# Lambda products of two batches as one full-height matmul, in an audio tower of signatures, a lambda layer and routed experts

## The chip, the cores and the metric

The kernel runs on one core of a Trainium2 chip. The metric is the device time of one execution in microseconds; lower is better. Everything that counts here is float32 (or fp32r, the same width read by TensorE in one pass instead of two).

## What is computed

The input is x, 64 sequences of 64 points with 7 channels. Three stages follow each other:

```
h = signature_features(x) @ W.T + b            # 64 x 63 tokens, 128 features
h = h + lambda_attention(layernorm(h))          # this stage is changed
h = h + routed_ffn(layernorm(h)) + shared_ffn   # 8 experts, top 1
```

The middle one, for each batch b of 63 tokens, has one key and one value head of 16 channels and 8 query heads:

```
q = bn(x @ Wq).reshape(b, 8, 16, t);  k = softmax((x @ Wk).reshape(b, 1, 16, t));  v = bn(x @ Wv).reshape(b, 1, 16, t)
lam_c = einsum('bukt,buvt->bkv', k, v)          # 16 x 16 per batch: the product that is changed
Yc = einsum('bhkt,bkv->bhvt', q, lam_c)
lam_p = relu(conv3x3(v, Wpos));  Yp = einsum('bhkt,bkvt->bhvt', q, lam_p)
out = (Yc + Yp) reshaped @ Wout + bout
```

## The kernel before, in words

The program has three blocks with a barrier between them: `signatures`, `middle` and `experts`. Only `middle` is touched. Each engine has its own instruction stream, in an order written out by hand; semaphores join them.

**Preparation in `middle`.** The raw keys and values come back from DRAM as 128 partitions x 8 groups (`G8`) x 63 tokens, where a group is 8 batches of 16 channels: `KR`/`KS` for keys, `VR`/`VN` for values. DVE normalizes the values, subtracts the maximum of the keys and later divides by their sum; ACT does the exponential. Then TensorE turns both so that tokens lie on partitions: `turn` makes 8 transposes of 128 x 63 into two PSUM banks each. ACT copies the banks into `VT` (63 x 64 batches x 16) and `KT` (63 x 64 x 16). At the same time the padded values are written to DRAM (`v_pad`) and read back as shifted images (`load_im`, tile `IM`) for the convolution; the first one must have landed before `conv(0, 0)`.

**The main loop.** `GB` = 4 batches make a group, so there are `NG` = 16 groups, and `step(k)` runs for k = -1 to 17. It is a software pipeline: step k works on the convolution and the attention of group k, on the layer norm and the shared FFN's first product of group g = k-1, and on the FFN's second product of group f = k-2. TensorE's order in a step is: `conv(k, 1)` (L1187), the second half of the sums of products of the group before (`add_products`, L1196), `conv(k, 2)`, the output projection (L1242), `down(f)` (L1218, 16 matmuls), `rank` in odd steps (L1226), `conv(k, 3)`, the content product (L1255), a transpose (L1262), `add_products(k, 0)`, the gate (L1270), `up(g)` (L1208, 12 matmuls), the **lambda product of group k+1** (L1279), and `conv(k+1, 0)`.

**The lambda product.** ACT repeats the 16 keys of each of 4 batches over 8 heads into `KH` (L976). TensorE makes one matmul for each batch, with `KH` of that batch as weights (63 rows, 128 columns) and `VT` of that batch as moving data (63 rows, 16 columns), into `psL`; the last one increments `lam_done`. ACT waits for that and copies `psL` to `LS` (L1001), and only then goes on to the GELUs of the group before (L963, L964). GpSimd makes `Gl` from `GF` (L912), which `down` waits for, and spreads `LS` over heads into `LC` (L916), which the content product waits for.

**The convolution** has 36 rows: `W36` and `IM` lie on partitions 0-35 for two of the batches and 64-99 for the other two. DVE's `products` (L1062, four in a row) wait for it, and `conv(k, 2)` waits until the first two of them have emptied a PSUM bank.

**DVE** ends even steps from k = 2 with `choose` (L1072 to L1080), which picks each token's expert and keeps the running counts `RUN`; it is in DVE's order ahead of the `products` of the next, odd step.

Of the kernel before, what the change touches and what calls it, by code (L numbers as in the profile page):

```python
# [6 lines left out]
f32 = mybir.dt.float32  # L7
# [4 lines left out]
ACT = mybir.ActivationFunctionType  # L12
AX = mybir.AxisListType

NB, S, F = 64, 63, 128
# [3 lines left out]
DK, NH = 16, 8  # L19
# [5 lines left out]
SP = 64  # L25
# [3 lines left out]
GB = 4  # L29
# [703 lines left out]
def middle(nc, m):  # L733
# [5 lines left out]
    with ExitStack() as ctx:  # L739
        def sb(name, shape, dt=f32):  # L740
            return ctx.enter_context(nc.sbuf_tensor(name, shape, dt))
# [4 lines left out]
        G8, IC, HV, CT = NB // 8, I // 128, DK // 2, 2 * TOK  # L746
# [3 lines left out]

        flat, n_k = W2[:].rearrange("p e i h f -> p (e i h f)"), G8 * S
        KR, KS = (flat[:, n * n_k:(n + 1) * n_k].bitcast(f32).rearrange("p (g s) -> p g s", g=G8) for n in range(2))
        VR = flat[:, 2 * n_k:2 * n_k + G8 * SP].bitcast(f32).rearrange("p (g s) -> p g s", g=G8)
# [5 lines left out]
        PQ = sb("PQ", [128, 2, S])  # L759
        KT, VT = sb("KT", [S, NB, DK]), sb("VT", [S, NB, 4, 4])  # L760
        KH = sb("KH", [S, 2, GB, NH, DK])
        WPh, WPm, W36 = sb("WPh", [100, 128], f32r), sb("WPm", [100, 128]), sb("W36", [100, 128], f32r)
# [54 lines left out]
        psV = PS[7][:, 0:2 * DK].rearrange("p (a c) -> p a c", a=2)  # L817
        psKT, psVT = PS[6:8], PS[4:6]

# [71 lines left out]
        def _(pool):  # L891
            L = Links(pool, pool_link)
            for x in (VN[:, :, 0:1], VN[:, :, SP:SP + 2]):
                pool.memset(x, 0.0).then_inc(vp_set, 1)
# [47 lines left out]
        def _(act):  # L942
# [6 lines left out]
            load_im(act, 0, (1,))  # L949

            act.wait_ge(kv_done, 1)
            for h in range(2):
                act.activation(VT[:, 32 * h:32 * h + 32], psVT[h][0:S, :].rearrange("p (b r j) -> p b j r", r=4, j=4), ACT.Copy).then_inc(kvt_ready, 1)
            act.wait_ge(kv_done, 2)
            for h in range(2):
                act.activation(KT[:, 32 * h:32 * h + 32].rearrange("p b k -> p (b k)"), psKT[h][0:S, :], ACT.Copy).then_inc(kvt_ready, 1)
            act.wait_ge(kvt_ready, 4)

# [7 lines left out]
            def step(k):  # L966
# [7 lines left out]
                if on(k + 1, 0, NG):  # L974
                    wait_from_one(act, lam_done, k)
                    act.activation(KH[:, w], KT[:, (k + 1) * GB:(k + 2) * GB].unsqueeze(2).broadcast_to([S, GB, NH, DK]),  # L976
                                   ACT.Copy).then_inc(kh_ready, 1)
# [180 lines left out]
        def _(pe):  # L1158
# [8 lines left out]

            def turn(to, x, lo):
                for q in range(G8):
                    ins = pe.transpose(to[q // 4][0:S, 128 * (q % 4):128 * (q % 4) + 128], x[:, q, lo:lo + S], ident)  # L1170
                ins.then_inc(kv_done, 1)
            pe.wait_ge(vn_ready, 2)
            turn(psVT, VN, 1)
            pe.wait_ge(k_ready, 1)
            turn(psKT, KS, 0)
            pe.wait_ge(w36_ready, 1)
# [52 lines left out]
            def step(k):  # L1229
# [43 lines left out]
                if on(k + 1, 0, NG):  # L1273

                    pe.wait_ge(kh_ready, k + 2)
                    if on(g, 0, NG):
                        pe.wait_ge(lg_ready, g + 1)
                    for b in range(GB):
                        ins = pe.matmul(psL[:, b], KH[:, w, b].rearrange("p h k -> p (h k)"), VT[:, (k + 1) * GB + b].rearrange("p j r -> p (j r)"), start=True, stop=True)  # L1279
                    ins.then_inc(lam_done, 1)  # L1280
# [3 lines left out]
            conv(0, 1)  # L1284
            pe.wait_ge(kvt_ready, 4)
            for k in range(-1, NG + 2):
# [216 lines left out]
```

## Time and profile before

| | |
|---|---|
| median of 3 executions | 672.87 us (669.7 to 681.77) |
| profiled execution, own time | 672.23 us |
| profiled execution, span | 670.3 us |
| mean granted clock of TensorE | 0.926 of full speed |
| busy: PE, PE weight loads, DVE, ACT, POOL | 89%, 72%, 75%, 42%, 45% |

The profiled execution's span is 1.9 us shorter than its own time; the rest lies around the program. Times in rows are microseconds from the span's start. `signatures` takes up to about 311, `middle` from there to about 523 with its tail, `experts` the rest.

### The profile page before, as it was taken

The page shows a single profiled execution, that of the slowest core. Times are in us where ns is not written, and L with a number is a line of the kernel's source. Part 1 is how long each engine was busy: PE and PEld are TensorE (multiplying, and loading weights), DVE is VectorE, ACT ScalarE, POOL GpSimd, SP SyncE. Part 2 cuts the span into 40 slices and gives each one's busy share as a digit, 9 for nine tenths or more (in the row PEclk, how much of TensorE's full clock was granted, in tenths as well). Part 3 has the DMA queues.
Part 4 walks back from the last instruction along what each step waited for, and adds up shares of the span by engine and source line. Part 5 has one row for each costly group of instructions (what it writes and reads, how often), then busy time and mean ns, then how long its engine had stood idle before and what let it go on. Part 6 is the DMA issues. An engine that isn't in the chain of part 4 may idle for free. (4 is left out here: it accounts for less than half of the span.)

```text
span 670.3 us, 13330 instructions
## 1 busy us (share of the span) xinstructions
PE 597.9 (89%) x3687; PEld 480.0 (72%) x3687; DVE 505.3 (75%) x1405; ACT 282.7 (42%) x692; POOL 302.3 (45%) x304
## 2 busy tenths in 40 slices
PE   2789999999999999992699999999998449999995
PEld 1468888888888888881466777777776338888884
DVE  6979889999999888867647788778776317777773
ACT  4323333333333333312235767566767125545451
POOL 3833335555555433200224677776765602333332
PEclk9799999999999999996557998989999659999998
DMA  8303566666665444455777665645540121222210
GB/s 290 23 1 114 164 188 187 190 191 189 190 190 174 160 160 160 160 161 152 115 163 110 101 131 126 117 88 117 101 89 25 50 69 44 68 67 72 62 58 9
DMA packets 130050, 80.89 MB, mean 121 GB/s; under 512 B 69428, under 2 KB 124365, under 8 KB 130006
## 3 DMA queue, kind: packets, MB, share of 16 engines
q1 hardware_dynamic: 125432, 73.75, 42.9%
q0 software_dynamic: 3296, 6.27, 3.1%
q10 hardware_dynamic: 1278, 0.32, 0.3%
q8 instruction: 23, 0.38, 0.2%
q14 instruction: 21, 0.17, 0.1%
HBM read 31.53 MB, written 49.33 MB: 121 GB/s over the span
## 5 line engine op out<-in xcount | busy, mean ns | idle before, releaser
L1062 DVE SCALAR_TENSOR_TENSOR P<-PS,QN 128x512 f32<-128x512 f32 x128 | 79.4, 683 | 33.4 <-PE PS L1187 33.4
L546 DVE SCALAR_TENSOR_TENSOR Z<-PS,Vt,Z 126x128 f32<-126x128 f32 x224 | 78.6, 351 | 8.7 <-PE PS L674 0.6
L1334 POOL DMA_INDIRECT out_h<-OS,XS x39 | 38.0, 974 | 92.1 <-DVE OS L1378 91.6
L674 PE MATMUL PS<-Wh,Ah 128*126 128x512 f32 x256 | 78.7, 430 | 0.0
L332 POOL TENSOR_TENSOR INCl<-INC,INCh 126x512 fp32r<-126x512 f32 x31 | 40.1, 1293 | 74.4 <-ACT INCh L409 74.4
L674 PE MATMUL PS<-Wl,Ah 128*126 128x512 f32 x256 | 70.5, 397 | 2.2 <-DVE Wl L510 2.2
L674 PE MATMUL PS<-Wh,Al 128*126 128x512 f32 x256 | 71.1, 400 | 0.0
L674 PEld LDWEIGHTS PS<-Wl,Ah 128*126 128x126 f32 x256 | 48.0, 188 | 14.9 <-issue 2.7
L674 PEld LDWEIGHTS PS<-Wh,Al 128*126 128x126 f32 x256 | 48.3, 189 | 12.5
L449 ACT ACTIVATE XT<-PS 128x126 f32<-128x126 f32 x32 | 8.9, 277 | 108.0 <-PE PS L720 108.0
L674 PEld LDWEIGHTS PS<-Wh,Ah 128*126 128x126 f32 x256 | 44.8, 192 | 7.8 <-issue 1.5
L369 POOL TENSOR_TENSOR W1l<-WRW,W1h 128x512 f32 x16 | 20.6, 1289 | 65.8 <-ACT W1h L459 65.8
L912 POOL TENSOR_TENSOR Gl<-GF,Gh 128x504 fp32r<-128x504 f32 x32 | 40.2, 1260 | 21.2 <-ACT GF L964 21.0
L1187 PE MATMUL PS<-IM,W 36*128 36x512 f32 x128 | 35.7, 516 | 10.9 <-DVE P L1062 6.2
L323 POOL TENSOR_TENSOR TOP<-A2T,Vhalf 126x512 f32 (+1 forms) x32 | 42.9, 1341 | 2.9 <-DVE A2T L487 2.7
L674 PE MATMUL PS<-WT,AT 128*126 128x512 f32 (+1 forms) x128 | 40.7, 398 | 2.4 <-DVE WT L537 2.4
L1410 PE MATMUL PS<-W,GTh 128*128 x156 | 41.9, 302 | 0.5 <-DVE GTl L1371 0.5
L1368 DVE TENSOR_TENSOR GX<-PS,SG 128x512 f32<-128x512 f32 x39 | 27.0, 692 | 20.1 <-PE PS L1396 20.1
L409 ACT ACTIVATE INCh<-INC 126x512 fp32r<-126x512 f32 x32 | 20.3, 633 | 50.2 <-DVE INC L491 50.2
L1218 PE MATMUL PS<-S,Gh 128*126 128x256 f32 x128 | 37.1, 321 | 3.7 <-POOL Gl L912 3.7
L1410 PE MATMUL PS<-W,GTl 128*128 x156 | 38.7, 281 | 0.0
L491 DVE TENSOR_TENSOR INC<-A2X,V 126x512 f32 (+1 forms) x32 | 38.5, 1203 | 0.1
(218 smaller groups left out, 1605.3 us busy)
## 6 DMA issues: line engine op xcount, KB each, us to landing
routed<-nobody SPq DMA_DIRECT2D x30, 1170.0 KB, 5.2
IM<-v_pad SPq DMA_DIRECT2D x62, 157.5 KB
XS<-routed SPq DMA_DIRECT2D x39, 130.0 KB, 2.2
WRW<-in_w SPq DMA_DIRECT2D x16, 256.0 KB, 3.1
R<-h_rows SPq DMA_DIRECT2D x16, 129.9 KB
W1l<-in_wsig SPq DMA_DIRECT2D x4, 512.0 KB, 8.6
WR<-in_w SPq DMA_DIRECT2D x8, 256.0 KB, 5.9
q_raw<-QS SPq DMA_DIRECT2D x32, 63.0 KB
```

The costliest lines, as they stand in the source:

```text
L323: pool.tensor_tensor(TOP[:, u].rearrange("p (a b) -> p a b", b=C), A2T[:, bass.ds(t, 1)].rearrange("p t a b -> p (t a b)").unsqueeze(2).br ...
L332: pool.tensor_tensor(INCl[:], INC[:], INCh[:].bitcast(f32), ALU.subtract).then_inc(incl_ready, 1)
L491: dve.tensor_tensor(INC[:].rearrange("p (a b) -> p a b", b=C), A2X[:, bass.ds(t, 1), 0:C2].rearrange("p t c -> p (t c)").unsqueeze(2).broa ...
L546: ins = dve.scalar_tensor_tensor(Z[:, u], psU[h][:, d], sc, Z[:, u], ALU.mult, ALU.add)
L674: ins = pe.matmul(out, a, w, start=(n == 0), stop=(n == len(turn) - 1))
L912: pool.tensor_tensor(Gl[:, hs], GF[:, hs], Gh[:, hs].bitcast(f32), ALU.subtract).then_inc(gl_ready, 1)
L1062: ins = dve.scalar_tensor_tensor(P[:, b, HV * h:HV * h + HV], psC[2 * pair + hb], 0.0, QN[:, g % 2, b:b + 1].broadcast_to([128, HV, SP]), ...
L1187: ins = pe.matmul(PS[2 * pair + hb][:, :], W36[r:r + 36], IM[r:r + 36, g % 2, VB * pair + HALF * h:VB * pair + HALF * h + HALF], start=Tru ...
L1218: ins = pe.matmul(psF[:, t].rearrange("p h f -> p (h f)"), a[:, i, TOK * t:TOK * t + TOK], S2[:, i].rearrange("p h f -> p (h f)"), start=( ...
L1334: pool.indirect_dma_start(out_rows, bass.IndirectOffsetOnAxis(XS[:, k % XB, IDC:IDC + 1].bitcast(i32), 0), OS[:, k % 2], None, bounds_chec ...
L1368: dve.tensor_tensor(GX[:, u], psU[u][1], SG[:, u], ALU.mult).then_inc(gx_ready, 1)
L1410: ins = pe.matmul(psY[u], a[:, u, i], W2[:, bass.ds(expert[k - 2], 1), i].rearrange("p e h f -> p (e h f)"), start=(i == 0 and p == 0), st ...
```

## The change

Two neighbouring batches share one matmul. The even batch's tokens lie on partitions 0-62 and the odd one's on 64-126, so that `KH` is 128 rows high and holds 2 pairs per group. `VT` becomes 128 x 32 pairs x 2 x 16: for a pair, the even batch's values are in the first 16 columns on the upper partitions, the odd batch's in the second 16 columns on the lower ones, and the rest is zero. One matmul of 128 rows and 32 columns then gives both batches' products side by side, and a group takes 2 instead of 4. To get there, `turn` no longer transposes: it multiplies by the columns of the identity that belong to the even batches (into partitions 0-63) and to the odd ones (64-127), 16 matmuls of 64 x 64 instead of 8 transposes, into one bank. GpSimd sets `VT` and a 64th key column to zero at the start. ACT makes one copy for `KT` instead of two, and `KH` is 128 x 256 instead of 63 x 512.

```diff
-        KT, VT = sb("KT", [S, NB, DK]), sb("VT", [S, NB, 4, 4])
-        KH = sb("KH", [S, 2, GB, NH, DK])
+        KT, VT = sb("KT", [128, NB // 2, DK]), sb("VT", [128, NB // 2, 2, 4, 4])
+        KH = sb("KH", [128, 2, GB // 2, NH, DK])
...
-            for x in (VN[:, :, 0:1], VN[:, :, SP:SP + 2]):
+            for x in (VN[:, :, 0:1], VN[:, :, SP:SP + 2], KSP[:, :, S:SP], VT[:]):
                 pool.memset(x, 0.0).then_inc(vp_set, 1)
...
+            act.wait_ge(vp_set, 4)
             act.wait_ge(kv_done, 1)
             for h in range(2):
-                act.activation(VT[:, 32 * h:32 * h + 32], psVT[h][0:S, :].rearrange("p (b r j) -> p b j r", r=4, j=4), ACT.Copy).then_inc(kvt_ready, 1)
+                act.activation(VT[64 * h:64 * h + 64, :, h], psVT[64 * h:64 * h + 64, :].rearrange("p (b r j) -> p b j r", r=4, j=4), ACT.Copy).then_inc(kvt_ready, 1)
             act.wait_ge(kv_done, 2)
-            for h in range(2):
-                act.activation(KT[:, 32 * h:32 * h + 32].rearrange("p b k -> p (b k)"), psKT[h][0:S, :], ACT.Copy).then_inc(kvt_ready, 1)
-            act.wait_ge(kvt_ready, 4)
+            act.activation(KT[:].rearrange("p b k -> p (b k)"), psKT[:, :], ACT.Copy).then_inc(kvt_ready, 1)
+            act.wait_ge(kvt_ready, 3)
...
-                    act.activation(KH[:, w], KT[:, (k + 1) * GB:(k + 2) * GB].unsqueeze(2).broadcast_to([S, GB, NH, DK]),
+                    act.activation(KH[:, w], KT[:, (k + 1) * GB // 2:(k + 2) * GB // 2].unsqueeze(2).broadcast_to([128, GB // 2, NH, DK]),
...
             def turn(to, x, lo):
+                ones = ident.rearrange("p (b h k) -> p h b k", h=2, k=DK)
                 for q in range(G8):
-                    ins = pe.transpose(to[q // 4][0:S, 128 * (q % 4):128 * (q % 4) + 128], x[:, q, lo:lo + S], ident)
+                    for h in range(2):
+                        ins = pe.matmul(to[64 * h:64 * h + 64, 64 * q:64 * q + 64], x[:, q, lo:lo + SP], ones[:, h], start=True, stop=True)
                 ins.then_inc(kv_done, 1)
+            pe.wait_ge(vp_set, 4)
...
-                    for b in range(GB):
-                        ins = pe.matmul(psL[:, b], KH[:, w, b].rearrange("p h k -> p (h k)"), VT[:, (k + 1) * GB + b].rearrange("p j r -> p (j r)"), start=True, stop=True)
+                    for b in range(GB // 2):
+                        ins = pe.matmul(psL[:, 2 * b:2 * b + 2], KH[:, w, b].rearrange("p h k -> p (h k)"),
+                                        VT[:, (k + 1) * GB // 2 + b].rearrange("p h j r -> p (h j r)"), start=True, stop=True)
                     ins.then_inc(lam_done, 1)
```

## Rows read from the trace of the kernel before

**Rows 1.** Busy time and granted clock (PEclk) by stretch of the main loop.
```profile
328.00:359.60 31.60, 31.44 (x163) 21.70 (x162) 17.20 (x39) 11.89 (x25) 10.49 (x12) 0.50 0.77 142
...
414.40:417.60 3.20, 3.20 (x16) 3.20 (x16) 2.28 (x10) 2.33 (x4) 2.81 (x4) 0.50 0.40 99
...
441.80:503.00 61.20, 59.85 (x543) 45.74 (x542) 47.46 (x138) 39.06 (x82) 41.84 (x44) 1.00 0.51 99
```

**Rows 2.** Timeline of ACT: the copy of lambda that ends each step (ends of steps 8 to 11).
```profile
435.33 0.22 ACT L1001 ACTIVATE LS<-PS 128x64 f32<-128x64 f32 x1 [0.61 <-PE PS L1279]
...
448.67 0.22 ACT L1001 ACTIVATE LS<-PS 128x64 f32<-128x64 f32 x1 [0.61 <-PE PS L1279]
...
459.40 0.22 ACT L1001 ACTIVATE LS<-PS 128x64 f32<-128x64 f32 x1 [0.62 <-PE PS L1279]
...
470.49 0.22 ACT L1001 ACTIVATE LS<-PS 128x64 f32<-128x64 f32 x1 [0.61 <-PE PS L1279]
```

**Rows 3.** Timeline around the start of step 8, an even one (brackets: idle before, and releaser).
```profile
423.28 0.28 PE L1208 MATMUL PS<-X2l,S1h 128*128 128x252 f32 x1
...
423.49 0.84 PE L1279 MATMUL PS<-VT,KH 63*128 63x16 f32 x6
...
424.08 0.50 PE L1187 MATMUL PS<-IM,W 36*128 36x512 f32 x1
...
424.41 0.71 PE L1187 MATMUL PS<-IM,W 36*128 36x512 f32 x3
...
425.03 2.48 DVE L1062 SCALAR_TENSOR_TENSOR P<-PS,QN 128x512 f32<-128x512 f32 x4 [2.88 <-PE PS L1187]
...
425.92 1.26 POOL L912 TENSOR_TENSOR Gl<-GF,Gh 128x504 fp32r<-128x504 f32 x1 [0.33 <-ACT GF L964]
...
426.18 0.38 ACT L973 ACTIVATE YC<-PS 128x252 f32<-128x252 f32 x1 [0.40 <-PE PS L1196]
...
426.80 0.70 PE L1242 MATMUL PS<-WO,YC 128*126 128x128 f32 x4
```

**Rows 4.** Timeline around the start of step 7, an odd one.
```profile
410.46 1.98 DVE L1080 TENSOR_TENSOR RUN<-RUN,OH 126x8 f32<-126x8 f32 x4
...
410.93 1.28 POOL L912 TENSOR_TENSOR Gl<-GF,Gh 128x504 fp32r<-128x504 f32 x1
...
413.73 0.50 PE L1187 MATMUL PS<-IM,W 36*128 36x512 f32 x2 [1.00 <-DVE P L1062]
```

**Rows 5.** Timeline of DVE around the start of step 11, a later odd one.
```profile
458.29 0.77 DVE L1080 TENSOR_TENSOR RUN<-RUN,OH 126x8 f32<-126x8 f32 x4
459.83 1.89 DVE L1062 SCALAR_TENSOR_TENSOR P<-PS,QN 128x512 f32<-128x512 f32 x3 [0.77 <-PE PS L1187]
```

**Rows 6.** Line 1279's weight loads alone: duration in ns, minimum/median/maximum.
```profile
L1279 PEld LDWEIGHTS PS<-VT,KH x128: 182/188/335, 328.1 to 502.8; 63*128 63x128 f32 x128
```

**Rows 7.** Timeline of the preparation, 312 to 328.
```profile
312.51 0.64 PE L1165 MATMUL PS<-K,BNP 128*32 128x128 f32 x4
...
318.23 1.97 PE L1170 MATMUL PS<-K,W 128*63 128x128 f32 x8 [5.08 <-DVE W L1024]
...
319.07 0.99 SPq L825 DMA_DIRECT2D IM<-v_pad  x2
...
322.85 1.07 ACT L956 ACTIVATE KT<-PS 63x512 f32<-63x512 f32 x2 [1.54 <-PE PS L1170]
...
323.95 0.63 ACT L976 ACTIVATE KH<-KT 63x512 f32<-63x512 f32 x1
...
327.54 1.22 PE L1187 MATMUL PS<-IM,W 36*128 36x512 f32 x4 [4.72 <-DMA IM<-v_pad]
```

**Rows 8.** A GpSimd memset of 384 elements per partition, at the program's start.
```profile
0.84 0.41 POOL L310 MEMSET AXs<- 126x384 f32 x1
```

**Rows 9.** Timeline, end of step 1: the load of the third image, and its convolution.
```profile
343.19 3.39 SPq L825 DMA_DIRECT2D IM<-v_pad  x4
...
352.39 1.39 PE L1187 MATMUL PS<-IM,W 36*128 36x512 f32 x4
```

More of the change, by code:

```diff
@@ L748, in middle @@
         P = sb("P", [128, GB, DK, SP])
-        flat, n_k = W2[:].rearrange("p e i h f -> p (e i h f)"), G8 * S
-        KR, KS = (flat[:, n * n_k:(n + 1) * n_k].bitcast(f32).rearrange("p (g s) -> p g s", g=G8) for n in range(2))
+        flat, n_k = W2[:].rearrange("p e i h f -> p (e i h f)"), G8 * SP
+        KR = flat[:, 0:G8 * S].bitcast(f32).rearrange("p (g s) -> p g s", g=G8)
+        KSP = flat[:, n_k:2 * n_k].bitcast(f32).rearrange("p (g s) -> p g s", g=G8)
+        KS = KSP[:, :, 0:S]
         VR = flat[:, 2 * n_k:2 * n_k + G8 * SP].bitcast(f32).rearrange("p (g s) -> p g s", g=G8)
@@ L817, in middle @@
         psV = PS[7][:, 0:2 * DK].rearrange("p (a c) -> p a c", a=2)
-        psKT, psVT = PS[6:8], PS[4:6]
+        psKT, psVT = PS[6], PS[4]
         def load_im(eng, g, cs=range(2)):
@@ L1174, in _ @@
             pe.wait_ge(k_ready, 1)
-            turn(psKT, KS, 0)
+            turn(psKT, KSP, 0)
             pe.wait_ge(w36_ready, 1)
@@ L1284, in _ @@
             conv(0, 1)
-            pe.wait_ge(kvt_ready, 4)
+            pe.wait_ge(kvt_ready, 3)
             for k in range(-1, NG + 2):
```

## The prediction

> **What bounds the kernel now.** I read busy time and clock by stretch first. From 328 to 503 TensorE is busy nearly all the time, at half its clock (0.50, the 1.2 GHz level) up to 359.6 and at full clock afterwards, but for two drops of 3.2 us each, of which one is shown [rows 1]. So the main loop hangs on TensorE's order, and the changed matmul stands in that order. Next come the steps' lengths: step 10 takes 459.40 - 448.67 = 10.73, step 11 takes 470.49 - 459.40 = 11.09, and step 9, which holds a drop of the clock, 13.34 [rows 2]. A share of busy time doesn't say what a shorter matmul is worth, so the third view is the timeline where one step passes into the next. There are two kinds of passage.
>
> Into an even step: DVE has been idle for 2.88 when its products start, and TensorE's convolution released it; that convolution is queued behind the lambda product [rows 3]. Here time saved on lambda moves everything. Into an odd step: DVE first finishes the choice of experts. In step 7 its four tiny count updates took 1.98 instead of the 0.77 of step 11, since one of them was held while GpSimd ran L912, and then it is TensorE that waits 1.00 for DVE [rows 4]. Time saved on lambda is lost there. In step 11 the updates were not held and DVE still waited 0.77 for the convolution [rows 5]; there the saving counts, as long as it is under 0.77. I looked at all passages: those into 4, 6, 8, 10, 12, 14 are of the first kind, those into 3, 5, 7, 9 of the second, those into 11, 13, 15 of the third.
>
> **The change, part by part.**
>
> *The lambda product.* A float32 matmul is two passes. Six passes of lambda take 0.84, of which the last one alone is 0.28 (the length of one record), so they start 0.84 - 0.28 = 0.56 over 5, or 0.112, apart [rows 3]. Such a pass moves only 16 columns but loads 128 columns of weights in 0.188 [rows 6]; the load sets the distance. 32 moving columns instead of 16 shouldn't change it, nor should 128 rows instead of 63. So 8 passes become 4: 4 x 0.112 = 0.45 less at full clock, 0.90 at half.
>
> Something is given back. One of the four convolution matmuls started at 424.08, while lambda still ran; it lies on the other half of the rows, and lambda with 128 rows leaves no half free. But the other convolutions could only start at 424.41, behind the last lambda pass, and DVE waited for one of these [rows 3]. So the overlap that is lost wasn't on the path. There is also a step in TensorE's layout: 423.28 to 423.49, or 0.21, from the last full-height matmul to the first half-height one, against 0.112 within lambda [rows 3]. It costs 0.1 and now comes behind lambda instead of ahead of it. I take between 0 and 0.1 more for that, and a net 0.40 a step (0.35 to 0.45).
>
> A rule of the Trainium skill speaks against the change here: TensorEngine Tiling (Array Packing), section Key Properties, says that going from one tiling mode to another drains the engine, and that tiles work independently of each other. By it, before the change lambda and convolution share a mode of 64 rows, and after it the switch lies between them; their number stays one. The trace agrees with the 0.21 above. By rule and row alike the sum would be the same but for these 0.1 a step, 0.9 in all.
>
> *Who is late next.* With convolution and DVE 0.40 earlier, `down` at 427.2 is next to GpSimd's L912, which ends at 425.92 + 1.26 = 427.18 and started 0.33 after GpSimd came free [rows 3]. ACT's copy of lambda stands ahead of the GELU that L912 waits for, so that one moves too, but by no more than those 0.33. In the three even steps like this one I take off 0.08 each, 0.2.
>
> *Full clock, sum.* Six even passages and three odd ones, 9 x 0.40 = 3.6, less 0.2: **3.4**. The four passages with a late DVE give 0; their saved 0.40 turns into more idle time of TensorE (1.00 becomes 1.4) [rows 4].
>
> *Half clock, steps 0 to 2.* Three lambda products would save 0.9 each, 2.7. But the third image sets a wall: the first image was asked for at 319.07 and used at 327.54, 8.5 later [rows 7]; the third one is asked for at 343.19, when the transfers before it allow, and so is there at about 351.7, and its convolution starts at 352.39 [rows 9]. So at most 0.7 are kept. If the clock then rises at the same moment as before, those 0.7 are worth half. I take **0.5** (0.35 to 2).
>
> *KH, a copy of half the width.* 0.62 before, for 512 columns; 252 columns take ACT 0.38 [rows 3]. It saves 0.24 on ACT, which is busy 42% and in these steps goes on to a table load for the layer norm. The transpose that needs its result comes after TensorE's own queue. Gain 0, bound 0.24 a step where ACT is late; I saw no place where that would end a step.
>
> *Turning keys and values.* Before, 8 passes each in 1.97. Afterwards 16 matmuls, 32 passes, with 64 weight columns and 64 moving ones. The four passes of L1165 (32 columns wide, on two different column groups) take 0.64 in all with 0.42 for one, so they go two by two: 0.42 + 0.22 [rows 7]. The halves of `turn` are on different column groups too. A pass of `turn` before moves 128 columns in (1.97 - 0.47) / 7 = 0.21, with 0.47 for the first, so 64 columns want 0.11; two by two that is 16 x 0.11 = 1.8 for each turn, as long as before, and one by one 3.5. The first turn begins at 318.23; the second ended at 322.85; the path through ACT is two copies (1.07) and `KH` (0.63), done at 324.6, while TensorE then waits for the image until 327.54 [rows 7]. Even one by one (1.5 more and another 1.5 more, less 0.5 for the copy saved and 0.24 on `KH`) it would be done at 326.9. So cost 0, under a cover of 3 us.
>
> *The memsets.* `VT` has 1024 columns. 384 took 0.41 [rows 8], so 1.1, early in the block, where GpSimd's next work comes at 319. The waits for `vp_set` on TensorE and ACT stand behind work that ends at 318 or later, so they find it done. If it held DVE as in rows 4, it would delay the first image by up to 1.1, half of which the third image's wall takes back. I take 0, range 0 to 1.1.
>
> **Sum.** 3.4 + 0.5 = 3.9. The profiled execution took 672.23 of its own, 1.9 more than its span, and lies 0.6 below the median of 672.87. 672.23 - 3.9 = 668.3 in its terms, **669.0** against the median.
>
> **The rivals.**
>
> *A. The slow clock lasts longer: slower than before.* The level rose at 359.6 only, though TensorE had been busy for 31.44 of 31.60 before [rows 1]; so busy time alone doesn't raise it, and it fell twice later in steps like step 7, with the idle 1.00 [rows 1, 4], which becomes 1.4. What 1 us at the half level costs: step 9 with a drop took 13.34, step 11 without one 11.09 [rows 2]; of these 2.2, up to 1.0 is the wait for DVE, so 1.2 to 2.2 for 3.2 us, some 0.55 each us. If the rise comes one step later (11 us), that is 6.0 more, 675.0. It decides from 3.9 / 0.55 = 7 us more of half level on, or from a third further drop. For it: the three executions before spread over 12 us, and the level is a thing that could differ between them. Against: the shift is small.
>
> *B. The clock rises sooner.* The same with the other sign: everything in steps 0 to 2 lies up to 0.7 earlier and has fewer passes between its long ones. 8 us less at 0.55: 4.4, so 664.6. The executions before reach down to 669.7, so the sign is open.
>
> *C. DVE is held in steps 10, 12 and 14 too.* There no update was held before [rows 5]; if the order of updates and L912 tips, a hold of 1.98 - 0.77 = 1.21 [rows 4, 5] eats the 0.77 of slack and puts 0.44 on TensorE, and the 0.40 are lost: 3 x 0.84 = 2.5, so 671.5. Both hang on the same chain of TensorE, which speaks against it.
>
> *D. The turns run one by one and at the distance of a full load.* At 0.21 a pass 32 passes take 6.8, twice, so they'd end at 331.9 and `KH` at 332.9; lambda then starts 4.8 later than at 328.1, and the third image gives back 0.7. About 4 lost: 673.
>
> *E. It doesn't do what it says.* If 128 rows cost twice what 63 do, 4 passes take as long as 8: gain nil, 672.9. Rows 3 show full-height L1242 (128 rows) at four passes in 0.70, which is 0.14 apart, so no.
>
> **Chances.** Forecast 0.55 (666 to 671); A 0.16; B 0.12; C 0.07; D 0.05; E 0.05. The range runs from B, with a little below it, to A: 662.5 to 677. About 2% is what a measurement of this kernel can tell from no change. Nothing above reaches 13 us; only A or B with more than one mechanism at a time would: faster by over 2% 0.04, slower by over 2% 0.05, within 0.91.
>
> **What would show it right.** Four passes of L1279 in each step, 0.11 apart; the odd and even passages as above, with even steps 0.4 shorter or the pair of steps 0.4 shorter up to step 9 and 0.8 after it; TensorE's idle time for DVE near 1.4 in steps 5, 7 and 9; each turn near 1.8; the first convolution still released by its image at 327.5. Wrong: a pass above 0.15 apart, a first convolution released by anything else than the image, or another length of the half level, which would drown the sum.

## The result, and the profile after

The kernel after the change takes **684.22 us** (median of 4 runs, 681.96 to 690.44) against 673.15 for the kernel before on the same chip (median of 4, 669.70 to 681.77): ratio **1.020**, interval 1.015 to 1.024. It is slower by 2%, where 0.6% faster was forecast, and lies outside the range given. The profiled execution took 690.44, its span 688.0. It was the slowest of the four, with a mean granted clock of 0.901 (0.910, 0.917 and 0.922 in the others), so what its trace shows of the slow clock is more than is usual for this kernel. Ratios here and below leave out executions that lie more than 1.5% above the fastest of their kernel, so they are not always the quotient of the two medians beside them.

The steps' ends come first, as in [rows 2]: ACT's copy of lambda in the timeline of the kernel after.

```profile
451.93 0.22 ACT L1003 ACTIVATE LS<-PS 128x64 f32<-128x64 f32 x1
...
468.69 0.23 ACT L1003 ACTIVATE LS<-PS 128x64 f32<-128x64 f32 x1
479.04 0.22 ACT L1003 ACTIVATE LS<-PS 128x64 f32<-128x64 f32 x1
489.59 0.23 ACT L1003 ACTIVATE LS<-PS 128x64 f32<-128x64 f32 x1
```

Step 9 takes 16.76 (before 13.34), step 10 10.35 (10.73) and step 11 10.55 (11.09). So most steps are shorter, as intended, and a few are much longer. All sixteen such rows in both traces give this, in us:

```
step     0     1     2     3     4     5     6     7     8     9    10    11    12    13    14    sum
before  7.15 15.35 13.58 11.57 10.73 11.82 10.72 13.40 10.74 13.34 10.73 11.09 10.73 11.15 10.72 172.8
after   6.81 14.52 13.25 19.30 12.15 16.41 10.35 16.65 10.38 16.77 10.34 10.55 10.20 10.54 10.21 188.4
```

Steps 3, 4, 5, 7 and 9 lose 20.4, of which 9.2 fall on steps 3 and 4; the ten others win 4.8. What happens in step 9 is in its timeline, which answers to [rows 3] and [rows 4] at once; brackets give the idle time before an instruction and who ended it. Kernel after:

```profile
451.24 1.00 POOL L904 DMA_INDIRECT routed<-R,POS  x1 [0.19 <-issue]
...
451.37 0.53 PE L1284 MATMUL PS<-VT,KH 128*128 128x32 f32 x4
...
451.81 4.82 DVE L1082 TENSOR_TENSOR RUN<-RUN,OH 126x8 f32<-126x8 f32 x4
...
451.82 0.74 PE L1192 MATMUL PS<-IM,W 36*128 36x512 f32 x4
...
452.27 2.48 POOL L914 TENSOR_TENSOR Gl<-GF,Gh 128x504 fp32r<-128x504 f32 x2
...
454.70 1.07 POOL L918 TENSOR_TENSOR LC<-LS,K 128x512 f32<-128x512 f32 x1
...
455.73 0.67 POOL L924 TENSOR_TENSOR QN<-QR,PQ 128x252 f32<-128x252 f32 x1
...
456.57 2.48 DVE L1064 SCALAR_TENSOR_TENSOR P<-PS,QN 128x512 f32<-128x512 f32 x4
...
457.92 0.79 PE L1192 MATMUL PS<-IM,W 36*128 36x512 f32 x2 [4.36 <-DVE P L1064]
```

The four lambda passes stand where they should, and then DVE needs 4.82 for four updates of `RUN` that move 8 columns each. In the kernel before it was 1.98 [rows 4], and 0.77 with none held [rows 5]. One of the four is held: by its own record it lasts from 452.22 to 456.43 here, 4.216, where a free one takes 0.17. That is the whole train of GpSimd, two times L914, L918 and L924, ending at 456.40. In the kernel before, the held update ended with the *first* of the two Gl instructions, and a gap came behind that one. One more row of the kernel before, from the passage of [rows 4]:

```profile
412.53 1.25 POOL L912 TENSOR_TENSOR Gl<-GF,Gh 128x504 fp32r<-128x504 f32 x1 [0.32 <-ACT GF L964]
```

GpSimd sat idle for 0.32 until ACT had the second half of `GF` ready, and in this gap DVE got its turn. With lambda earlier, ACT's copy `LS` and the GELU behind it come earlier too, the second half of `GF` is there when GpSimd wants it, and the gap is gone. The products of step 9 then start at 456.57, TensorE waits 4.36 for them (before 1.00), and the clock falls while it waits. Stretches of the kernel after, columns as in [rows 1]:

```profile
451.93:457.93 6.00, 1.64 (x22) 0.62 (x22) 5.90 (x7) 3.88 (x9) 5.70 (x7) 0.82 0.48 99
457.93:463.93 6.00, 6.00 (x30) 5.28 (x30) 3.88 (x14) 1.78 (x3) 0.50 (x1) 0.61 0.11 31
463.93:468.69 4.76, 4.75 (x48) 3.87 (x48) 2.87 (x8) 1.89 (x5) 2.63 (x3) 1.00 0.55 88
```

TensorE is busy for 1.64 of the first six us, and runs the next six, in which it is busy throughout, at a granted 0.61, a mixture of the two levels. Half clock within the main loop adds up to 65.7 us, against 36.2 before.

Steps 5, 7 and 9 all look like this (holds of 4.219, 4.220, 4.216). Step 3 does not:

```profile
366.57 2.76 DVE L1082 TENSOR_TENSOR RUN<-RUN,OH 126x8 f32<-126x8 f32 x4
...
366.84 2.47 POOL L914 TENSOR_TENSOR Gl<-GF,Gh 128x504 fp32r<-128x504 f32 x2 [1.02 <-ACT GF L966]
...
369.26 1.09 POOL L918 TENSOR_TENSOR LC<-LS,K 128x512 f32<-128x512 f32 x1
```

The two Gl and L918 run without a gap here too, and yet two updates are held for 1.15 and 1.17, one behind each Gl, and DVE is free when L918 starts. TensorE waits 2.27, and half clock follows from 370.5 to 391.0, which makes steps 3 and 4 the dearest pair of this execution. From step 11 on nothing is held: the last update has started (479.18) before Gl starts, since GpSimd there still waits for ACT. Kernel after, step 11:

```profile
478.58 0.77 DVE L1082 TENSOR_TENSOR RUN<-RUN,OH 126x8 f32<-126x8 f32 x4
478.93 0.73 PE L1192 MATMUL PS<-IM,W 36*128 36x512 f32 x4
479.20 2.52 POOL L914 TENSOR_TENSOR Gl<-GF,Gh 128x504 fp32r<-128x504 f32 x2 [1.08 <-ACT GF L966]
```

The preparation went as forecast; these rows answer to [rows 7] and [rows 8], and its last to [rows 9]:

```profile
313.83 0.95 POOL L896 MEMSET VT<- 128x1024 f32 x1
...
320.48 1.98 PE L1174 MATMUL PS<-K,W 128*64 128x64 f32 x32 [5.17 <-DVE W L1026]
...
323.23 1.97 PE L1174 MATMUL PS<-K,W 128*64 128x64 f32 x32 [0.77 <-DVE W L1052]
...
325.88 0.42 ACT L978 ACTIVATE KH<-KT 128x256 f32<-128x256 f32 x1
...
329.86 1.22 PE L1192 MATMUL PS<-IM,W 36*128 36x512 f32 x4 [4.66 <-DMA IM<-v_pad]
...
354.89 0.73 PE L1192 MATMUL PS<-IM,W 36*128 36x512 f32 x4 [1.49 <-DMA IM<-v_pad]
```

The loop's 15.6 and a first block that was 2.2 longer in this execution make 17.8 of the 18.2 between the two profiled executions. The medians differ by 11.

### The profile page after: what moved, and what is told of

The parts are those of the page before. It is cut to its first block and busy times, and to the rows that moved or that the text cites. A ratio compares the mean times of both kernels' runs of the same rounds, so it can differ in the third digit from the quotient of the medians.

```text
span 688.0 us, 13301 instructions
## 1 busy us (share of the span) xinstructions
PE 602.3 (88%) x3671; PEld 482.5 (70%) x3671; DVE 515.8 (75%) x1405; ACT 278.8 (41%) x691; POOL 302.3 (44%) x306
## 5 line engine op out<-in xcount | busy, mean ns | idle before, releaser
L1064 DVE SCALAR_TENSOR_TENSOR P<-PS,QN 128x512 f32<-128x512 f32 x128 | 79.3, 682 | 33.9 <-PE PS L1192 33.9
L674 PE MATMUL PS<-Wl,Ah 128*126 128x512 f32 x256 | 72.7, 407 | 3.2 <-DVE Wl L510 3.2
L674 PEld LDWEIGHTS PS<-Wl,Ah 128*126 128x126 f32 x256 | 49.4, 193 | 16.2 <-issue 3.6
L1192 PE MATMUL PS<-IM,W 36*128 36x512 f32 x128 | 32.4, 545 | 24.3 <-DVE P L1064 18.0
L914 POOL TENSOR_TENSOR Gl<-GF,Gh 128x504 fp32r<-128x504 f32 x32 | 39.8, 1263 | 16.3 <-ACT GF L966 16.1
L1223 PE MATMUL PS<-S,Gh 128*126 128x256 f32 x128 | 39.8, 337 | 3.7 <-POOL Gl L914 3.7
L1201 PE MATMUL PS<-P,K 128*32 128x256 f32 x512 | 38.6, 424 | 0.0
```

The costliest lines, as they stand in the source:

```text
L674: ins = pe.matmul(out, a, w, start=(n == 0), stop=(n == len(turn) - 1))
L914: pool.tensor_tensor(Gl[:, hs], GF[:, hs], Gh[:, hs].bitcast(f32), ALU.subtract).then_inc(gl_ready, 1)
L1064: ins = dve.scalar_tensor_tensor(P[:, b, HV * h:HV * h + HV], psC[2 * pair + hb], 0.0, QN[:, g % 2, b:b + 1].broadcast_to([128, HV, SP]), ...
L1192: ins = pe.matmul(PS[2 * pair + hb][:, :], W36[r:r + 36], IM[r:r + 36, g % 2, VB * pair + HALF * h:VB * pair + HALF * h + HALF], start=Tru ...
L1201: ins = pe.matmul(psY[32 * j:32 * j + 32], K[:, K_BD + 24 - 8 * r:K_BD + 56 - 8 * r], P[:, :, 4 * r + j], start=False, stop=(r == 3))
L1223: ins = pe.matmul(psF[:, t].rearrange("p h f -> p (h f)"), a[:, i, TOK * t:TOK * t + TOK], S2[:, i].rearrange("p h f -> p (h f)"), start=( ...
```

## The experiments

Three theories stood after the first look. **H:** the held update alone costs the time. **L:** something in the new lambda format (128 rows, the lost overlap with the convolution) costs it. **A:** the clock falls because four passes fewer in a step leave TensorE less busy. A fourth was added after experiment 3, **C:** the clock, which falls once TensorE waits for DVE, costs a share of its own. Times are medians.

**1. Close the gap in the kernel before.** Kernel before; ACT makes its copy of lambda behind the pair of GELUs that opens a step (the second half of the group) instead of ahead of it. The product is untouched.

```
  in ACT's step(k), behind gelu(f, 1):
+     act.wait_ge(lam_done, k + 1)
+     ...
+     act.activation(LS[:], psL..., ACT.Copy).then_inc(ls_ready, 1)
  at the end of the step:
-     act.wait_ge(lam_done, k + 2)
-     ...
-     act.activation(LS[:], psL..., ACT.Copy).then_inc(ls_ready, 1)
```

> The kernel before, with one swap on ACT: the copy of lambda (LS) comes behind the first pair of GELUs of the step instead of ahead of it. No work is added or removed anywhere, TensorE's order and the layouts stay. Theory H (the hold): a small DVE instruction with two SBUF inputs can't start while GpSimd runs tensor instructions back to back, and what the change did was to close the 0.3 us gap between GpSimd's two L912. This swap closes the same gap. H expects single count updates (RUN) of about 4.2 us in steps 4, 6 and 8 as in the changed kernel (1.38 before), TensorE waiting over 4 us for DVE at conv(k, 2), more of the half clock, and 680 to 688 us. Theory A (less activity: the clock falls because lambda's removed passes make TensorE less busy): nothing changes, updates of 1.38 us at most and 673 us, within 3. Theory L (the full-height layout or the turn costs): the same, 673.

**686.41** (685.59 to 687.18), ratio 1.024 (1.017 to 1.032). The timeline of its step 9:

```profile
444.72 4.82 DVE L1080 TENSOR_TENSOR RUN<-RUN,OH 126x8 f32<-126x8 f32 x4
...
445.17 2.48 POOL L912 TENSOR_TENSOR Gl<-GF,Gh 128x504 fp32r<-128x504 f32 x2
...
450.82 0.79 PE L1187 MATMUL PS<-IM,W 36*128 36x512 f32 x2 [3.84 <-DVE P L1062]
```

Two lines of order on ACT make the old kernel as slow as the new one, with the same 4.82 on DVE and step 9 at 16.55. The new product isn't needed for the loss; L falls as its main cause. So does A: no pass is gone, and half clock in the loop is 53.4 against 36.2.

**2. Issue the new product twice.** Kernel after, each of the two lambda matmuls issued a second time with the same result.

```
-                    for b in range(GB // 2):
+                    for b in (0, 1, 0, 1):
```

> The changed kernel with both lambda matmuls of a group issued twice into the same place (same result), so TensorE spends 8 passes again. H expects the GELUs as late as before the change, the gap open by about 0.3 us, the longest update at 1.4 us and 671 to 676 us. A expects the same time, since the activity is back; so this one tells both from L, which expects 684 or more (the layout and the turn are unchanged and passes are added).

**669.80** (669.33 to 674.89), ratio 0.997 (0.993 to 1.001): a little under the time expected, more work on TensorE, and 14 us less than the kernel after. Timeline of its step 7:

```profile
410.50 1.98 DVE L1082 TENSOR_TENSOR RUN<-RUN,OH 126x8 f32<-126x8 f32 x4
...
410.97 2.67 POOL L914 TENSOR_TENSOR Gl<-GF,Gh 128x504 fp32r<-128x504 f32 x2
...
413.77 0.50 PE L1192 MATMUL PS<-IM,W 36*128 36x512 f32 x2 [1.08 <-DVE P L1064]
```

Two Gl instructions now take 2.67 instead of 2.48: the second starts 0.14 behind the first one's end (0.14 to 0.16 in steps 5, 7 and 9), where in the kernel after their records touch. With this gap the hold is back at 1.38. The new format by itself costs nothing that shows.

**3. Do the gap's job with ACT.** Kernel after; two idle copies on ACT (640 columns) behind `LS`.

```
+                    act.activation(JK[:, 0:512], KT[:]..., ACT.Copy)
+                    act.activation(JK[:, 512:640], KT[:, 0:8]..., ACT.Copy)
```

> The changed kernel, with two idle copies on ACT (512 and 128 columns into a tile that nobody reads) behind the copy of lambda, which delay the GELUs by about 0.7 us and so open the gap between GpSimd's two L914 again. TensorE's work is that of the changed kernel. H expects the longest update back at about 1.4 us, the wait of TensorE for DVE back near 1 us, and 668 to 674 us. A expects the clock to stay as low as in the changed kernel, and L the loss to stay: 681 to 686, or more by the ACT work.

**682.25** (681.30 to 684.57), ratio 1.019 (1.010 to 1.028): a miss for H alone, and the time that A and L expected. The holds are back at 1.37 and TensorE waits only 1.51 in step 9, and yet that step takes 18.54:

```profile
437.61 1.97 DVE L1085 TENSOR_TENSOR RUN<-RUN,OH 126x8 f32<-126x8 f32 x4
...
440.86 0.79 PE L1195 MATMUL PS<-IM,W 36*128 36x512 f32 x2 [1.51 <-DVE P L1067]
```

Its stretch over the whole of step 9 shows where the time is: granted clock 0.58, TensorE busy for 17.03 of 18.54.

```profile
437.72:456.26 18.54, 17.03 (x96) 13.41 (x96) 9.80 (x26) 8.18 (x20) 9.95 (x11) 0.58 0.49 85
```

Half clock in the loop is 55.1 us. How much of it follows such a wait varies: in this execution steps 5 and 7 had waits of 1.52 and 1.51 too, with 3.4 us of half clock each, and took 13.4; in experiment 2 waits of 1.06 to 1.09 had none behind them.

**4. The same, with dummy work in the wait.** Ten matmuls whose result nobody reads, ahead of conv(k,2) in steps 3, 5, 7, 9.

```
+                pe.wait_ge(ls_ready, k + 1)   # in steps 3, 5, 7, 9
+                for _ in range(10):
+                    pe.matmul(PS[7][:, 256:512], W1h[:, 0, I:I + 128], W1h[:, 0, 0:256], start=True, stop=True)
```

> The kernel of e5 (changed, with ACT delayed so that GpSimd's gap is open again; 682.25) had the hold back at 1.37 us and still kept the loss; its TensorE waited 1.3 to 1.5 us for DVE in steps 3, 5, 7, 9 (1.0 before, where two of three such waits were followed by the half clock) and the half clock came in each of 5, 7, 9. Here ten matmuls of 128 x 256 columns, whose result nobody reads, fill that wait in the four steps; nothing else differs. Theory C (what is left after the hold is the clock alone: TensorE has too little to do around the wait): no drop of the clock after 362 up to the end of the loop, steps 5, 7, 9 at 11.9 us, step 10 at 10.8, and 669 to 674 us. Theory W (the added ACT work costs it): 682, or more by the filling.

**670.04** (669.77 to 670.49), ratio 0.999 (0.995 to 1.002). DVE's updates still take 1.96, nothing of use was added, and 12 us are gone. Its step 9, with 11.87 instead of 18.54, and the fill in it:

```profile
432.42:444.29 11.87, 11.74 (x106) 9.17 (x106) 9.71 (x26) 8.18 (x19) 8.97 (x10) 1.00 0.59 105
```

```profile
433.98 1.46 PE L1243 MATMUL PS<-W1h 128*128 128x256 f32 x10
435.56 0.50 PE L1196 MATMUL PS<-IM,W 36*128 36x512 f32 x2
```

So C has a share: what an idle TensorE costs here is above all the clock after it. L, whose format is untouched by the fill, can't account for these 12 us. W has a small share: with and without the fill, the even steps without half clock take 10.8 against 10.35 in the kernel after.

**5. Fill alone in the kernel after.** The same fill, 12 in step 3 and 36 in steps 5, 7, 9, with the hold left as it is.

> The changed kernel, hold of 4.2 us and all, with matmuls whose result nobody reads in TensorE's waits for DVE: 36 in steps 5, 7, 9 (3.9 us at full clock), 12 in step 3. It separates the hold's direct price from the clock's. If most of the loss is the clock's, steps 5, 7, 9 go from 16.4-16.8 to 14.9 us (6.0 up to conv(k, 2) and 8.85 behind it), step 4 to 10.3, the half clock after 360 goes and the time is 672 to 678 us. If the hold's late DVE costs it all by itself, 682 to 686.

**675.97** (674.34 to 677.11), ratio 1.007 (1.003 to 1.011). No half clock after step 2; holds still 4.25 to 4.27; steps 5, 7, 9 take 14.7 to 14.8. This splits the loss in such a step: 16.41 to 16.77 with hold and clock, 14.8 with the hold alone, 11.1 with neither (next run). Some 3.7 are the late DVE, 1.6 to 2.0 the clock. In steps 3 and 4 the clock is the larger part: 19.30 and 12.15 become 12.59 and 10.21. Step 3 of the kernel after, with its clock of 0.60, for comparison:

```profile
366.69:385.98 19.29, 17.02 (x96) 13.40 (x96) 10.55 (x26) 7.57 (x17) 7.58 (x8) 0.60 0.64 87
```

Between the two traces the loop differs by 14.5; in the medians, where the kernel after has less of the slow clock than in its trace, the fill is worth 8.3.

**6. Take away the cause.** Kernel after; GpSimd waits for the updates before its first Gl in odd steps.

```
+                    if k % 2 and k >= 3:
+                        pool.wait_ge(run_ready, (k - 3) // 2 + 2)
                     for h in range(2):
```

> The changed kernel with one wait more: in odd steps GpSimd doesn't start its first L914 before DVE has finished the count updates of the choice (run_ready). H expects no update over 0.4 us, TensorE released into conv(k, 2) with no more than 0.3 us of waiting for DVE, L914 and down later by 0.4 to 0.6 us in steps 5, 7, 9, and 660 to 667 us, faster than both kernels. A expects the clock of the changed kernel and 680 or more; L 680 or more as well.

**662.56** (660.49 to 663.75), ratio 0.987 (0.979 to 0.995). It is 22 us faster than the kernel after and beats both. Timeline of its step 7:

```profile
430.28 0.77 DVE L1084 TENSOR_TENSOR RUN<-RUN,OH 126x8 f32<-126x8 f32 x4
...
431.14 2.49 POOL L916 TENSOR_TENSOR Gl<-GF,Gh 128x504 fp32r<-128x504 f32 x2 [0.43 <-ACT Gh L967]
...
432.34 0.49 PE L1194 MATMUL PS<-IM,W 36*128 36x512 f32 x2 [0.31 <-DVE P L1066]
```

GpSimd gives up 0.43 (the bracket names the GELU that ended last, at 431.11, but this Gl needs only the one before; the updates ended at 431.05). DVE's updates are back at 0.77, and TensorE waits 0.31. Half clock in the loop is 23.4 with the passes still gone, which speaks against A once more.

**7. The same wait in the kernel before.**

> The kernel before with the wait of e2 (GpSimd's first L912 of an odd step waits for the count updates). The hold of 1.38 us in steps 5, 7, 9 and 1.15 in step 3 goes, those steps come to 11.2 to 11.6 us at full clock (11.57, 11.82, 13.40, 13.34 before), TensorE waits at most 0.3 us for DVE, and the time is 666 to 670 us: the wait helps both, and the difference to e2 (662.6) is then what the change itself is worth, some 4 to 5 us.

**667.99** (665.69 to 668.76), ratio 0.995 (0.991 to 0.999). The old kernel had the same fault in small.

**8. Both once more, on one chip.** The kernels of 6 and 7 (e9 and e10 in the texts), 6 and 8 executions, so that their difference is the change alone with the held update out of the way.

> The kernel after the change with GpSimd's wait for run_ready ahead of the first Gl instruction in odd steps from 3, a second time, on one chip with its partner e10. All theories that the earlier runs left: no update of RUN is held over 0.2 us, the clock stays at its full level from step 3 on, and the time is 660 to 665 us. Against e10 the difference is the change by itself, with neither held update: I expect 4 to 6 us (the forecast's own sum was 3.9; steps 4 to 14 of the earlier two profiles give 0.37 to 0.55 apart each).

> The kernel before the change with the same wait of GpSimd, a second time, on the chip of e9. Expected 666 to 669 us, 0.990 to 0.999 of the kernel before, with steps 5, 7 and 9 at 11.1 instead of 11.8 to 13.4.

**662.34** (659.89 to 664.70; ratio 0.987, 0.982 to 0.992) and **665.76** (664.17 to 667.14; 0.991, 0.988 to 0.994): the change by itself is worth **3.4 us**, a little under the 4 to 6 expected (the two ranges overlap by 0.5), and in the loops of the two traces 4.15:

```
step              0     1     2     3     4     5     6     7     8     9    10    11    12    13    14    sum
before + wait   7.14 15.34 13.74 11.13 10.73 11.13 10.72 11.12 10.72 11.09 10.72 11.11 10.73 11.06 10.71 167.2
after + wait    6.81 14.06 14.55 11.16 10.18 11.09 10.36 11.15 10.34 11.11 10.36 10.77 10.20 10.70 10.21 163.1
```

**9. Half of the product left out.** Kernel before, lambda of batches 0 and 2 of each group of four only; the content product of the other two is missing.

```
-                    for b in range(GB):
+                    for b in (0, 2):
```

> The kernel before with two of the four lambda matmuls of a group left out (batches 1 and 3 of each group get no content product, so the output is not the reference's). Layouts, turn, KH and memsets are those of before; only TensorE's four passes of a step are gone, as in the change. If the loss comes from the time saved on lambda (the gap between the two L912 closes), this kernel shows the 4.2 us updates, over 4 us of waiting at conv(k, 2) and 680 to 687 us, like the changed one. If the full-height layout or the turn had a part in the loss, it lies 3 us or more under the changed one (684.2).

**679.92** (672.45 to 682.97), ratio 1.010 (1.002 to 1.017). The trace is of the slowest of the four executions, 682.97. Four passes fewer in the old format make even steps 10.29 to 10.35 instead of 10.73 (step 8, with half clock in it, 12.03), and steps 3, 5, 7 and 9 13.1 to 19.6. So the four passes' time, without their new form, sets it off. But the median lies 4.3 under the kernel after, and by the text above (3 or more) this would leave the format a part in the loss. The trace has another reason for it: of three passages with the scatter ahead and no gap between the two Gl, only the one into step 5 has a hold of the whole train, 4.23. In steps 7 and 9 it is 1.37 + 1.17, one update behind each Gl. Step 9:

```profile
445.42 1.00 POOL L902 DMA_INDIRECT routed<-R,POS  x1 [0.19 <-issue]
...
445.99 2.98 DVE L1080 TENSOR_TENSOR RUN<-RUN,OH 126x8 f32<-126x8 f32 x4
...
446.45 2.48 POOL L912 TENSOR_TENSOR Gl<-GF,Gh 128x504 fp32r<-128x504 f32 x2
...
448.88 1.08 POOL L916 TENSOR_TENSOR LC<-LS,K 128x512 f32<-128x512 f32 x1
```

That the format costs less than the four passes bring is shown by experiment 8, where the kernel that has it is the faster one.

**10. Can the slow start be had too?** The kernel of 6 (e11) with 18 unread matmuls while TensorE waits for the first image and 10 in step 1.

> e9 with 18 unread products (128 rows of weights, 256 columns) where TensorE waits for the first image, and 10 more in step 1 where it waits for the third. If the half clock of steps 0 to 2 (23.4 us of it in the loop of the earlier profile) is what holds them, the clock rises sooner and these steps lose up to 8 us, time 655 to 659. If the images' arrival is what holds them (TensorE waited 3.01 us for the third image in step 1 of that profile), the wait in step 1 grows by what step 0 and step 1 save, and the time falls by 0 to 3 us, 660 to 662. I take the second. The rival that fill itself delays: up to 1 us slower than e9.

**662.99** (660.39 to 665.53), ratio 0.989 (0.984 to 0.994): nothing. Steps 0 to 2 take 34.97 together, against 35.42 without the fill, although the half clock in the loop is down from 27.2 to 20.5. The mechanism is not the one that the text took. In its trace TensorE doesn't wait for the third image at all (1.55 in experiment 8). The ten matmuls take 2.50 at half clock, the layer norm's input comes later by them, and TensorE then waits for that:

```profile
340.28 2.50 PE L1190 MATMUL PS<-W1h 128*128 128x256 f32 x10
...
347.95 0.68 PE L1279 MATMUL PS<-K,R 126*128 126x126 f32 x2 [2.04 <-DVE R L1121]
```

Step 1 is longer by 3.3, step 2 shorter by 4.4. Whether the clock or the images hold these steps is not shown by this run.

**11. Which DVE instructions are held?** Kernel after, each update with one tensor in place of two. All counts become constants, so rows are placed elsewhere and the expert stage works on other rows.

```
-                    ins = dve.tensor_tensor(RUN[:, 4 * m + t + 1], RUN[:, 4 * m + t], oh[:, t], ALU.add)
+                    n = 4 * m + t + 1
+                    ins = dve.tensor_scalar(RUN[:, n], RUN[:, n - 1 if n < NT else 0], 1.0 if n < NT else 4.0, None, ALU.add)
```

> The kernel after the change, with each update of RUN made by an operation with one input in SBUF (it adds a constant, RUN[n] = RUN[n-1] + 1) in place of the sum of RUN and OH, which has two. The counts that the experts get are then constants, so rows are placed elsewhere and the expert stage works on other rows; nothing else is changed, and GpSimd has the same work at the same places. Theory one, it is the two SBUF inputs of a DVE operation that are held behind GpSimd's tensor instructions: no update takes over 0.2 us though GpSimd's L914, L914, L918, L924 still run beside it, TensorE waits 0.3 us or less at conv(k,2) in steps 5, 7, 9, the steps 3 to 9 take 11.1 and 10.3, no half clock after step 2, and the main loop is 163 to 165 us as in the kernel with GpSimd's wait. Theory two, any DVE operation that starts while GpSimd runs is held, whatever its inputs: the updates still take 4.2 us and the main loop 188 us. I take the first. The time of the whole is about 662 by the first and 684 by the second, give or take what other counts do in the expert stage.

**684.11** (681.23 to 698.29), ratio 1.016 (1.012 to 1.020). My theory one fell; the time and the hold are those of theory two. The timeline of its step 5:

```profile
387.22 1.00 POOL L904 DMA_INDIRECT routed<-R,POS  x1 [0.18 <-issue]
...
387.79 5.43 DVE L1083 TENSOR_SCALAR RUN<-RUN 126x8 f32<-126x8 f32 x4
...
388.25 2.47 POOL L914 TENSOR_TENSOR Gl<-GF,Gh 128x504 fp32r<-128x504 f32 x2
...
394.47 0.79 PE L1193 MATMUL PS<-IM,W 36*128 36x512 f32 x2 [4.94 <-DVE P L1064]
```

A `tensor_scalar` from SBUF to SBUF is held as well, 4.18 behind the same train, and 0.40 behind the scatter L904 ahead of it, which the sum of two tensors passed at its 0.17. Theory two, as I put it, fell as well, since other forms run beside GpSimd undelayed. In the kernel after, 73 of the 128 products L1064 (one input in PSUM) started while a GpSimd tensor instruction ran and took 0.67 to 0.69, as did the 55 others; the `tensor_reduce` L1074 takes 0.17 beside L935, and the comparison of two tensors L1075, right behind it, 0.54 to 0.78 instead of 0.19:

```profile
449.77 1.27 POOL L935 TENSOR_TENSOR W<-WR,W 128x512 fp32r<-128x512 f32 x1
...
450.35 0.17 DVE L1074 TENSOR_REDUCE lmax<-LG 126x4 f32<-126x32 f32 x1
...
450.56 0.54 DVE L1075 TENSOR_TENSOR eq<-LG,lmax 126x32 f32<-126x32 f32 x1
```

A `tensor_scalar` of the kernel after, L1118, agrees: 0.38 to 0.60 in seven cases beside a GpSimd tensor instruction, 0.33 to 0.35 in the 21 others. Of the forms in this loop, then, a `tensor_tensor` or a `tensor_scalar` between SBUF tensors is held; those with an operand in PSUM and the reductions are not. The Trainium skill, SBUF — State Buffer, section SBUF: two separate sides, says that DVE and GpSimd share one pair of ports, and that an operation with two SBUF inputs (against a GpSimd operation that reads SBUF), or one in a two-port mode, takes it whole and otherwise waits. The runs agree for two SBUF inputs. That the `tensor_scalar` ran in a two-port mode no view shows, but it was held, and by the scatter too, which the first kind passed. What that section doesn't say is shown by the 4.22: a wait can outlast the first GpSimd instruction and take in the whole train. It doesn't always. In the traces with a hold there are eighteen passages with no gap between the two Gl. In thirteen the hold was 4.18 to 4.27 (steps 5, 7 and 9 of the kernel after and of experiments 1, 5 and 11, step 5 of experiment 9); in five an update was held behind the first Gl alone and the next one behind the second (step 3 of the kernel after and of experiments 1 and 5, steps 7 and 9 of experiment 9). What decides between the two stays open. With a gap between the two Gl (0.09 was the shortest), no hold in any trace was longer than 1.39.

## Why the prediction was wrong

**The step that failed** is in "Who is late next", with what rests on it. I had the row: L912 started 0.33 after GpSimd came free, and the copy of lambda stands ahead of the GELU that it waits for, "so that one moves too, but by no more than those 0.33" [rows 3]. I read those 0.33, the gap between the two Gl of an even step, as slack that limits a gain of 0.08 a step. I didn't ask what moves in the odd steps, where the same gap stands between the two Gl (0.32) and is the time in which DVE gets its turn behind the held update. From this follows the next sentence, "The four passages with a late DVE give 0; their saved 0.40 turns into more idle time of TensorE (1.00 becomes 1.4)". It became 4.36 to 4.38 in steps 5, 7 and 9, which lost 4.6, 3.3 and 3.4 instead of 0, and 2.27 in step 3. I had priced the hold at one L912, 1.21, as if that were its nature; once the gap is closed it can take in GpSimd's whole train, here 4.05 above a free update's. Experiments 1, 2 and 6 show this from three sides: close the gap in the old kernel and it is slow, open it by 0.14 to 0.16 in the new one and it is well, order the two engines and it is better than either.

**Full clock, sum: 3.4.** Right where nothing is held. Passes at full clock started 0.109 to 0.112 apart, as in [rows 3], apart from a first distance of 0.03 in twelve of the sixteen steps. With the wait in both kernels, even steps from 4 on lose 0.36 to 0.55 and steps 11 and 13 0.34 and 0.36, against my 0.40; steps 3, 5, 7 and 9 win nothing (+0.03, -0.04, +0.03, +0.02), as said of them, but with TensorE waiting 0.31 and not 1.4. The idle overlap with the convolution cost nothing: leaving four passes out of the old kernel gives 0.44, the same.

**Half clock, 0.5.** Steps 0 to 2 gave 0.8 in the pair with the wait, and the wall is there as described: in the kernel after TensorE waited 1.49 for the third image. Experiment 10 doesn't tell whether the clock holds these steps as well. The sum of 3.9 for the change by itself was thus near the 3.4 of experiment 8; what it left out was the hold and the clock.

**The turns, KH, the memsets: 0.** Right. Each turn is 32 passes in 1.98 and 1.97 (1.8 forecast, 1.97 before), so they do run two by two; KH fell from 0.63 to 0.42 at no effect; the memset took 0.95 (1.1); the first convolution is still released by its image, after a wait of 4.66 (4.72 before).

**Rival A** came true in what it says of the clock, and not in its cause. It named 7 us more half level as the point from which it decides; there were 29.5. But I had put the trigger in the end of the first slow stretch, or in an idle time of 1.4, and took up to six us for it. What happened is the hold, and the clock behind it: experiment 5 puts the clock's part at 8.3 in the medians. My 0.55 for each us of half level overrates it there: between the traces of the kernel after and of experiment 5 it is 14.5 of loop for 45.6 of half level (65.7 against 20.1), or 0.32. **Rival C** had the right mechanism in the wrong steps (10, 12, 14, where nothing was held) and the wrong size (1.21). B, D and E: no sign of them; E is refuted by the passes' distance.

The two chances that together made 0.23, a longer half level (A) and an update held in more places (C), are one chain, and I had treated them as two small things. With its rows in hand, the sum was one question away: what else of GpSimd's stands right behind L912? L912 again, L916 and L922. [rows 4] had the first L912 with 1.28 and the timeline the others with 1.25, 1.08 and 0.68, 4.3 in all.

## What to carry to other kernels

When a small DVE operation between SBUF tensors takes much longer than its like, don't book the excess as its price: look at what GpSimd runs beside it, and count the whole train up to GpSimd's next idle time, since the hold can become that long if anything upstream gets faster (it did in thirteen of eighteen passages here). An idle time of a fraction of a us on an engine off the path can be what lets another engine through; before a step is shortened, list such gaps and ask which close. And where TensorE comes to wait for another engine (1.0 to 4.4 here), weigh the clock as well as the wait; ordering the two engines by one semaphore was worth more here (3 to 6 us in the kernel before, by the two ratios of 0.995 and 0.991, and 22 in the one after) than the shorter product (3.4).

## What was unexpected of the hardware

- A DVE `tensor_tensor` of 8 columns was held for 4.22 instead of 0.17, through four GpSimd instructions of 1.28, 1.25, 1.07 and 0.67 that ran back to back; with a gap of 0.14 to 0.16 between the first two it was 1.37 to 1.39. In five of eighteen passages without a gap DVE got its turn between the two all the same; why stays open. A `tensor_scalar` was also held, by an indirect DMA's instruction too (0.40).
- Behind the same wait of TensorE (1.51 and 1.51) the clock's fall cost one step 1.5 and another 6.7, in one execution (13.40 and 18.54 against 11.85 and 11.87 with the fill). Why the level came back late in one of them stays open.
- The kernel before spread over 669.35 to 686.99 in the thirteen runs beside experiment 8, and with GpSimd's wait over 664.17 to 667.14 in eight on that chip. That the hold makes this spread is likely, but no trace of a long execution of that kernel was taken, so it is not shown.
